# Gated cross-attention block with a mixture layer: the dense layer's rows rounded in row layout and turned by DMA transposes, logits one tile ahead

## The chip, the cores and the metric

One Trainium2 chip, one of its cores. The time is device microseconds of one execution of the whole program, input loads and output stores among them; it is the median of three executions.

## The reference, cut to what matters

```python
# x: (8, 512, 2048) f32, ctx: (8, 512, 2048) f32
x = x + tanh(g_xattn) * autocorrelation(layernorm(x), ctx, ctx)      # 8 heads, FFTs, top 12 lags
n = layernorm(x).reshape(-1, 2048)                                   # 4096 rows
base = n @ W_base.T + b_base                                         # W_base (2048, 2048)
gate = softmax(n @ W_gate.T)                                         # 8 experts
thr = sigmoid(n @ W_thr + b_thr) / 8
w = maximum(gate - thr, 0);  w = w / (sum(w) or 1)
h = einsum('nd,erd->ner', n, A_w)                                    # rank 16 for each expert
moe = einsum('ner,ne,eor->no', h, w, B_w) * 2
out = x + tanh(g_ffn) * (base + moe)
```

## The kernel before

The program has two stages in one launch. The first (the attention, to about 1545 us of the span) works through 32 steps of one batch row and 512 channels and writes the attention's result to a scratch tensor in HBM, `x2_scratch`. The change does not touch it. The second is the dense layer, and every line number below is of it.

**Weights.** `W_base`, `A_w`, `W_gate` with `W_thr`, and `B_w` are loaded in rows (into `row` and `wrow`, two 128x2048 f32 buffers each), transposed by TensorE into PSUM, and kept in SBUF as two fp16 parts each: the rounded value (`w_hi`, `ag_hi`, `b_hi`, made by ScalarE) and the remainder (`w_lo`, `ag_lo`, `b_lo`, made by VectorE). There are 19 jobs of four banks each. `ag` holds the 128 columns of `A_w`, 8 of the gate and 1 of the threshold, 137 in all.

**Tiles.** The 4096 rows are worked through in 32 tiles of 128 rows (`ROWS`), two buffers of `row` in turn. The first two and the last two tiles are written out, the others run in a loop that holds two tiles (`tiles`). There is no planner: the order on each engine is the order of the calls in its `step`. Products are taken as three fp16 products, hi·hi, hi·lo and lo·hi.

For tile i, TensorE does `logits(i)` (48 matmuls of 137 columns into `logit_bank`), `base(i)` (192 matmuls of 512 columns into the four banks of `dense`, which stay open), `turn_hw(i)` (one transpose of the gated `hw`), `turn(i + 1, 0, 2)` (8 transposes of the next tile's normalised rows into `turn_bank`), `experts(i)` (12 matmuls of 512 columns that add to `dense` and close it) and `turn(i + 1, 2, 4)` (8 more transposes). `experts(i)` needs `hwt_hi` (ScalarE) and `hwt_lo` (VectorE), both made out of the transposed `hw`. The first matmuls of `base(i)` wait, bank by bank, for `out_ready`: VectorE must have read the previous tile's result out of that bank in `finish`.

ScalarE: `gating(i)`, `normalise(i + 1, ...)` (square root, then a 128x2048 activation from `row` to `norm`), `hw_hi(i)`, `turned_hi(i + 1)` (four copies of a bank of `turn_bank` to `nt_hi`). VectorE: `gating(i)`, `statistics(i + 1, ...)`, `hw_lo(i)`, `turned_lo(i + 1, 0, 2)`, `finish(i)` (four operations, one for each bank of `dense`, into `row`), `turned_lo(i + 1, 2, 4)`. GpSimd adds the bias to `row` once tile i is normalised. SP, which issues all DMAs, in each step loads the next tile's `row` (after the store of the tile that had the buffer), waits for `out_ready`, and stores `row` to the output.

`nt_hi` and `nt_lo` have one buffer each, so they are overwritten only after `base_made`. `norm` has one buffer also.

## Time and profile before

| | |
|---|---|
| time, median of 3 executions | 3187.2 us (3184.11 to 3187.93) |
| the profiled execution | 3184.85 us |
| its span, first to last instruction | 3183.1 us |
| granted TensorE clock, mean over the span | 0.988 of full speed |
| TensorE matmul busy | 3033.0 us, 95% |
| VectorE, ScalarE, GpSimd busy | 1775.2, 873.3 and 1365.8 us |
| DMA queue q1 | 266.61 MB, 30.0% of 16 engines |

The busy time of TensorE counts each matmul to its modelled end, and matmuls overlap, so 95% is not 95% of its peak. The granted clock is 1.0 at 2.4 GHz and 0.5 at 1.2 GHz. Both stages are in the span; the shares are means over the two. In the profile's rows a line number such as L922 is a line of the kernel before.

### The profile page before, as it was taken

The numbers are of one execution on the slowest core, as the hardware profiler recorded it, in microseconds if no ns is written. First come the engines' busy times: TensorE is split into PE (matmuls) and PEld (weight loads), VectorE is DVE, ScalarE is ACT, GpSimd is POOL, SyncE is SP. The second block draws the span as 40 slices with busy tenths as digits, with TensorE's granted clock in tenths as the row PEclk, the third lists the DMA queues.
The fourth block names the chain that finished last, engine by engine and source line by source line (L and its number), as shares of the span: only waits on it lengthen the run. The fifth ranks groups of instructions, "written<-read, shape, count | busy, mean of one in ns | idle before, by whom it ended". The sixth has DMA issues, their size and how long they took to land.

```text
span 3183.1 us, 37157 instructions
## 1 busy us (share of the span) xinstructions
PE 3033.0 (95%) x13008; PEld 1569.3 (49%) x13008; DVE 1775.2 (56%) x2991; ACT 873.3 (27%) x1351; POOL 1365.8 (43%) x550
## 2 busy tenths in 40 slices
PE   4999999999999999998599999999999999999999
PEld 2545454555445455554454554545545545455454
DVE  4999999999999999888641222212212222122121
ACT  3343334333433344332421211211112112111120
POOL 4888887888888788884211101001011010110110
PEclk8999999999999999999899999999999999999999
DMA  9445544454445444431520111101101111011010
GB/s 213 124 114 124 134 111 116 121 138 105 120 122 139 104 118 113 113 83 40 219 99 27 53 40 40 53 26 53 53 26 53 40 40 53 26 53 53 26 53 27
DMA packets 130725, 267.52 MB, mean 84 GB/s; under 512 B 33705, under 2 KB 33833, under 8 KB 119881
## 3 DMA queue, kind: packets, MB, share of 16 engines
q1 hardware_dynamic: 130642, 266.61, 30.0%
q8 instruction: 28, 0.46, 0.1%
q14 instruction: 55, 0.45, 0.0%
HBM read 199.44 MB, written 67.11 MB: 84 GB/s over the span
## 4 chain that ended last, share of the span: by engine, by line
PE 50%; DMA 1%; DVE 0%; ACT 0%; issue 0%; DVEq 0%; ACTq 0%
PE bank L922 42%; PE bank L900 2%; PE bank L911 1%; PE bank L937 1%; PE bank L912 1%; PE bank L913 1%; PE bank L939 1%; PE bank L938 1%; PE bank L888 1%; DMA row<-in_L_ffn_W_base_dram 0%; DMA row<-in_L_ffn_A_w_dram 0%; DVE w_lo L1020 0%; PE bank L930 0%; DVE stats L1026 0%; ACT norm L971 0%
## 5 line engine op out<-in xcount | busy, mean ns | idle before, releaser
L1122 POOL TENSOR_TENSOR row<-row,bias 128x2048 f32<-128x2048 f32 x32 | 144.2, 4506 | 1426.8 <-ACT norm L971 1350.5
L720 POOL TENSOR_TENSOR spec_o<-spec_o,term 128x1024 f32<-128x1024 f32 x256 | 594.5, 2353 | 29.2 <-DVE term L558 29.2
L1082 DVE TENSOR_TENSOR hwt_lo<-bank,hwt_hi 128x128 f16<-128x128 f32 x32 | 9.3, 291 | 994.3 <-ACT hwt_hi L999 994.3
L922 PE MATMUL bank<-w_hi,nt_hi 128*128 128x512 f16 x2048 | 525.7, 379 | 0.0
L922 PE MATMUL bank<-w_hi,nt_lo 128*128 128x512 f16 x2048 | 525.6, 379 | 0.0
L922 PE MATMUL bank<-w_lo,nt_hi 128*128 128x512 f16 x2048 | 525.5, 379 | 0.0
L381 PE MATMUL bank<-wt,table 128*128 128x512 f32 x1024 | 448.2, 596 | 21.7 <-DVE prod_b L535 15.9
L381 PEld LDWEIGHTS bank<-wt,table 128*128 128x128 f32 x1024 | 192.2, 190 | 258.8 <-issue 229.8
L922 PEld LDWEIGHTS bank<-w_lo,nt_hi 128*128 128x128 f16 x2048 | 200.3, 98 | 241.7
L922 PEld LDWEIGHTS bank<-w_hi,nt_lo 128*128 128x128 f16 x2048 | 200.3, 98 | 241.6
L922 PEld LDWEIGHTS bank<-w_hi,nt_hi 128*128 128x128 f16 x2048 | 199.2, 98 | 234.2
L999 ACT ACTIVATE hwt_hi<-bank 128x128 f16<-128x128 f32 x32 | 8.9, 277 | 916.3 <-PE bank L930 916.3
L350 PE MATMUL bank<-qf,table 128*128 128x512 f32 x512 | 230.6, 604 | 16.2 <-POOL qf L701 13.0
L406 PE MATMUL bank<-spec_o,table 128*128 128x512 f32 x512 | 227.7, 597 | 14.6 <-POOL spec_o L720 10.9
L393 PE MATMUL bank<-table,prod_a 128*128 128x256 f32 x1024 | 229.0, 382 | 7.2 <-POOL prod_a L707 7.2
L393 PEld LDWEIGHTS bank<-table,prod_a 128*128 128x128 f32 x1024 | 196.4, 192 | 48.4 <-issue 14.8
L350 PEld LDWEIGHTS bank<-qf,table 128*128 128x128 f32 x512 | 99.2, 194 | 142.7 <-issue 141.3
L406 PEld LDWEIGHTS bank<-spec_o,table 128*128 128x128 f32 x512 | 97.8, 192 | 139.2 <-issue 123.9
L466 ACT ACTIVATE halves<-bank 128x1024 f32<-128x1024 f32 x32 | 32.7, 1023 | 454.7 <-PE bank L393 454.7
L685 POOL TENSOR_TENSOR v_sym<-vt 128x1024 f32<-128x1024 f32 x32 | 75.9, 2371 | 180.5 <-DVE corr L603 168.8
L1026 DVE BATCH_NORM_STATS2 stats<-row 128x6 f32<-128x512 f32 x124 | 76.6, 681 | 64.6 <-DMA row<-x_scratch 64.6
L701 POOL TENSOR_TENSOR qf<-xt 128x1024 f32<-128x1024 f32 x32 | 105.5, 3296 | 0.0
(149 smaller groups left out, 4428.5 us busy)
## 6 DMA issues: line engine op xcount, KB each, us to landing
xt<-in_x_dram SPq DMA_DIRECT2D x32, 1024.0 KB, 12.8
row<-x_scratch SPq DMA_DIRECT2D x32, 1024.0 KB, 4.8
out_dram<-row SPq DMA_DIRECT2D x32, 1024.0 KB, 3.9
xstat<-in_x_dram SPq DMA_DIRECT2D x28, 1024.0 KB, 10.7
vt<-in_ctx_dram SPq DMA_DIRECT2D x256, 64.0 KB
vt<-in_ctx_dram SPq DMA_DIRECT2D x64, 256.0 KB
xres<-in_x_dram SPq DMA_DIRECT2D x256, 64.0 KB
xres<-in_x_dram SPq DMA_DIRECT2D x64, 256.0 KB
```

What stands on the lines that cost most here:

```text
L350: mm = pe.matmul(pair(four, half)[:, row, :], q_tab[:, 2 * half + row, j, :], qf[:, 2 * row + j, :], start=(j == 0), stop=(j == 1))
L381: mm = pe.matmul(pair((mine, other)[y], half)[:, row, :], w_tab[:, 2 * half + row, j, :], wt[:, 2 * y + j, :], start=(j == 0), stop=(j == 1))
L393: mm = pe.matmul(four[:, ct, row * HALF:(row + 1) * HALF], prod_a[:, slot, ct * 128:(ct + 1) * 128], p_tab[:, slot, :], start=(half == 0), ...
L406: mm = pe.matmul(to[:, part, :], o_tab[:, slot, :], spec_o[:, h, slot, :], start=(row == 0), stop=(row == 1))
L466: act.activation(odd_part, four[:, :, HALF:C], ACT.Copy).then_inc(odd_copied, 1)
L685: pool.tensor_tensor(v_sym[:, 0:2, :], vt[:, 0:2, :], vt[:, 2:4, :], ALU.add).then_inc(v_symmed, 1)
L701: pool.tensor_tensor(qf[:, 2:4, :], xt[:, 0:2, :], xt[:, 2:4, :], ALU.subtract).then_inc(q_folded, 1)
L720: pool.tensor_tensor(to, to, term[:, buffer], sign).then_inc(term_added, 1)
L900: mm = pe.transpose(turn_bank[q % 2][:, k * 128:(k + 1) * 128], norm[:, d:d + 128], ident[:, :])
L922: mm = pe.matmul(dense[o][:, :], a[:, k, :], w[:, k, o * 512:(o + 1) * 512], start=(k == 0 and n == 0), stop=False)
L1026: op = dve.bn_stats(stats[:, q, :], x2[:, q * C:(q + 1) * C])
L1122: pool.tensor_tensor(row[:, par, :], row[:, par, :], bias[:, :], ALU.add).then_inc(bias_added, 1)
```

## The change

The transposes of the normalised rows leave TensorE. A tile's rows are loaded from `x2_scratch` a second time, into `norm` (`load_norm`), two tiles ahead; statistics and the normalising activation work in `norm` in place. ScalarE rounds `norm` to fp16 in row layout (`norm_hi`), GpSimd makes the remainder (`norm_lo`), and SP issues two DMA transposes, SBUF to SBUF, 128x2048 fp16 each, into `nt(par, part)`. There are two such pairs of tiles now; one pair and the two row-layout parts lie in the memory of `wrow`, which the weights no longer need by then. TensorE's step is `base(i)`, `turn_hw(i)`, `logits(i + 1)`, `experts(i)`. `turned_hi`, `turned_lo`, `turn` and `turn_bank` are gone. GpSimd adds the bias as soon as `row` is loaded. SP's steps are written out instead of looped. Left out below: renamed semaphores, the removed `turned_lo`, and unchanged lines.

```diff
@@ -750,8 +750,17 @@
             ag_hi, ag_lo = sb("ag_hi", [128, KD, NG], f16), sb("ag_lo", [128, KD, NG], f16)
             b_hi, b_lo = sb("b_hi", [128, D], f16), sb("b_lo", [128, D], f16)
             row = sb("row", [128, 2, D])
-            wrow = sb("wrow", [128, 2, D])
-            nt_hi, nt_lo = sb("nt_hi", [128, KD, 128], f16), sb("nt_lo", [128, KD, 128], f16)
+            wrow_mem = sb("wrow", [128, 2 * D])
+            wrow = wrow_mem[:, :].rearrange("p (a c) -> p a c", a=2)
+            nt_mem = sb("nt", [128, 2, KD, 128], f16)
+
+
+            spare = wrow_mem[:, :].bitcast(f16).rearrange("p (a k t) -> p a k t", a=4, k=KD)
+            norm_hi, norm_lo = (spare[:, a].rearrange("p k t -> p (k t)") for a in range(2))
+
+            def nt(par, part):
+                return spare[:, 2 + part] if par else nt_mem[:, part]
+
             bias = sb("bias", [128, D])
             ln2_scale, ln2_bias = sb("ln2_scale", [128, 1]), sb("ln2_bias", [128, 1])
             stats, mv = sb("stats2", [128, NCH, 6]), sb("mv2", [128, 2])
-            first_loaded = sem("first_loaded")
+            norm_loaded = sem("norm_loaded")
+            nt_loaded = [sem("nt_loaded0"), sem("nt_loaded1")]
+            norm_hi_made, norm_lo_made = sem("norm_hi_made"), sem("norm_lo_made")
             x2_loaded = [sem("x2_loaded0"), sem("x2_loaded1")]
             out_stored = [sem("out_stored0"), sem("out_stored1")]
-            normed, turned, nt_hi_made, nt_lo_made = sem("normed"), sem("turned"), sem("nt_hi_made"), sem("nt_lo_made")
+            normed = sem("normed")
-            dense, turn_bank, logit_bank, hw_bank = bank[0:4], bank[4:6], bank[6], bank[7]
+            dense, logit_bank, hw_bank = bank[0:4], bank[6], bank[7]
...
@@ -849,6 +860,20 @@
                     sp.dma_start(bias[:, :], b_base.rearrange("(a n) -> a n", a=1).to_broadcast([128, D])).then_inc(small_loaded, 16)
                     sp.dma_start(thr_b[:, :], b_thr.to_broadcast([128, 1])).then_inc(small_loaded, 16)
 
+                    def load_norm(i):
+                        sp.wait_ge(norm_hi_made, i)
+                        sp.wait_ge(norm_lo_made, i)
+                        sp.nop(nofuse=True)
+                        sp.dma_start(norm[:, :], x2_rows[i]).then_inc(norm_loaded, 16)
+
+                    def turn(i, par):
+                        if fleast(i) >= 2:
+                            sp.wait_ge(base_made, i - 1)
+                        for part, (source, made) in enumerate(((norm_hi, norm_hi_made), (norm_lo, norm_lo_made))):
+                            sp.wait_ge(made, i + 1)
+                            sp.nop(nofuse=True)
+                            sp.dma_start(nt(par, part), source, transpose=True).then_inc(nt_loaded[par], 16)
+
                     def load(i, par):
                         if fleast(i) >= 2:
                             sp.wait_ge(out_stored[par], 16 * (i // 2))
@@ -857,15 +882,21 @@
 
                     def step(i, par):
                         if fmost(i) + 1 < ROWS:
+                            turn(i + 1, 1 - par)
+                        if fmost(i) + 2 < ROWS:
+                            load_norm(i + 2)
+                        if fmost(i) + 1 < ROWS:
                             load(i + 1, 1 - par)
                         sp.wait_ge(out_ready, 4 * (i + 1))
                         sp.nop(nofuse=True)
                         sp.dma_start(out_rows[i], row[:, par, :]).then_inc(out_stored[par], 16)
 
-                    sp.wait_ge(wt_made, 4 * (JOBS - 1))
+                    turn(0, 0)
+                    load_norm(1)
+                    sp.wait_ge(wt_made, 4 * JOBS)
                     load(0, 0)
-                    sp.wait_ge(wt_made, 4 * JOBS)
-                    tiles(sp, step)
+                    for i in range(ROWS):
+                        step(i, i % 2)
                     for par in range(2):
                         sp.wait_ge(out_stored[par], 16 * ROWS // 2)
 
@@ -888,38 +919,24 @@
                                 mm = pe.transpose(view[:, k, :], source[0:rows, d:d + 128], ident[0:rows, 0:rows])
                             mm.then_inc(wt_made, 1)
 
-                    def turn(i, first, last):
-                        if first == 0:
-                            pe.wait_ge(normed, i + 1)
-                        for q in range(first, last):
-                            if q >= 2 or fleast(i) >= 1:
-                                pe.wait_ge(nt_hi_made, 4 * i + q - 1)
-                                pe.wait_ge(nt_lo_made, 4 * i + q - 1)
-                            for k in range(4):
-                                d = (4 * q + k) * 128
-                                mm = pe.transpose(turn_bank[q % 2][:, k * 128:(k + 1) * 128], norm[:, d:d + 128], ident[:, :])
-                            mm.then_inc(turned, 1)
-
-                    def logits(i):
+                    def logits(i, par):
                         if fleast(i) >= 1:
                             pe.wait_ge(logits_copied, i)
+                        pe.wait_ge(nt_loaded[par], 32 * (i // 2 + 1))
                         acc = logit_bank[:, 0:NG]
                         for k in range(KD):
-                            if k % 4 == 0:
-                                pe.wait_ge(nt_hi_made, 4 * i + k // 4 + 1)
-                                pe.wait_ge(nt_lo_made, 4 * i + k // 4 + 1)
-                            pe.matmul(acc, nt_hi[:, k, :], ag_hi[:, k, :], start=(k == 0), stop=False)
-                            pe.matmul(acc, nt_hi[:, k, :], ag_lo[:, k, :], start=False, stop=False)
-                            mm = pe.matmul(acc, nt_lo[:, k, :], ag_hi[:, k, :], start=False, stop=(k == KD - 1))
+                            pe.matmul(acc, nt(par, 0)[:, k, :], ag_hi[:, k, :], start=(k == 0), stop=False)
+                            pe.matmul(acc, nt(par, 0)[:, k, :], ag_lo[:, k, :], start=False, stop=False)
+                            mm = pe.matmul(acc, nt(par, 1)[:, k, :], ag_hi[:, k, :], start=False, stop=(k == KD - 1))
                         mm.then_inc(logits_made, 1)
 
-                    def base(i):
+                    def base(i, par):
                         for k in range(KD):
-                            for n, (a, w) in enumerate(((nt_hi, w_hi), (nt_hi, w_lo), (nt_lo, w_hi))):
+                            for n, (part, w) in enumerate(((0, w_hi), (0, w_lo), (1, w_hi))):
                                 for o in range(4):
                                     if k == 0 and n == 0 and fleast(i) >= 1:
                                         pe.wait_ge(out_ready, 4 * (i - 1) + o + 1)
-                                    mm = pe.matmul(dense[o][:, :], a[:, k, :], w[:, k, o * 512:(o + 1) * 512],
+                                    mm = pe.matmul(dense[o][:, :], nt(par, part)[:, k, :], w[:, k, o * 512:(o + 1) * 512],
                                                    start=(k == 0 and n == 0), stop=False)
                         mm.then_inc(base_made, 1)
 
@@ -940,18 +957,15 @@
                               .then_inc(dense_made, 1)
 
                     def step(i, par):
-                        logits(i)
-                        base(i)
+                        base(i, par)
                         turn_hw(i)
                         if fmost(i) + 1 < ROWS:
-                            turn(i + 1, 0, 2)
+                            logits(i + 1, 1 - par)
                         experts(i)
-                        if fmost(i) + 1 < ROWS:
-                            turn(i + 1, 2, 4)
 
                     pe.wait_ge(wt_hi, 4 * JOBS)
                     pe.wait_ge(wt_lo, 4 * JOBS)
-                    turn(0, 0, 4)
+                    logits(0, 0)
                     tiles(pe, step)
 
                 @block.scalar
@@ -962,22 +976,20 @@
                             act.activation(weight_target(g // 4, g % 4, 0), weight_bank(g // 4, g % 4), ACT.Copy,
                                            scale=W_SCALE).then_inc(wt_hi, 1)
 
-                    def normalise(i, x2):
+                    def normalise(i):
                         act.wait_ge(ln2_step, LN2_OPS * i + 3)
                         act.activation(std[:, :], var[:, :], ACT.Sqrt).then_inc(ln2_sqrt, 1)
                         act.wait_ge(ln2_step, LN2_OPS * (i + 1))
+                        act.activation(norm[:, :], norm[:, :], ACT.Identity, bias=ln2_bias[:, :],
+                                       scale=ln2_scale[:, :]).then_inc(normed, 1)
+
+                    def rounded(i, par):
+                        act.wait_ge(normed, i + 1)
                         if fleast(i) >= 1:
-                            act.wait_ge(turned, 4 * i)
-                        act.activation(norm[:, :], x2[:, :], ACT.Identity, bias=ln2_bias[:, :],
-                                       scale=ln2_scale[:, :]).then_inc(normed, 1)
-
-                    def turned_hi(i):
-                        if fleast(i) >= 1:
-                            act.wait_ge(base_made, i)
-                        for q in range(4):
-                            act.wait_ge(turned, 4 * i + q + 1)
-                            act.activation(nt_hi[:, 4 * q:4 * q + 4, :].rearrange("p k t -> p (k t)"),
-                                           turn_bank[q % 2][:, :], ACT.Copy).then_inc(nt_hi_made, 1)
+                            act.wait_ge(nt_loaded[1 - par], 32 * ((i - 1) // 2 + 1))
+                        else:
+                            act.wait_ge(wt_made, 4 * (NW + 1))
+                        act.activation(norm_hi, norm[:, :], ACT.Copy).then_inc(norm_hi_made, 1)
 
                     def gating(i):
                         act.wait_ge(logits_made, i + 1)
@@ -1000,16 +1012,17 @@
 
                     def step(i, par):
                         gating(i)
-                        if fmost(i) + 1 < ROWS:
-                            normalise(i + 1, row[:, 1 - par, :])
+                        if fmost(i) + 2 < ROWS:
+                            normalise(i + 2)
+                            rounded(i + 2, par)
                         hw_hi(i)
-                        if fmost(i) + 1 < ROWS:
-                            turned_hi(i + 1)
 
                     weights_hi(0, 4 * EARLY)
-                    normalise(0, norm)
+                    normalise(0)
                     weights_hi(4 * EARLY, 4 * JOBS)
-                    turned_hi(0)
+                    rounded(0, 0)
+                    normalise(1)
+                    rounded(1, 1)
                     tiles(act, step)
 
                 @block.vector
@@ -1021,9 +1034,11 @@
                                                      scalar=W_SCALE, in1=weight_target(g // 4, g % 4, 0), op0=ALU.mult,
                                                      op1=ALU.subtract).then_inc(wt_lo, 1)
 
-                    def statistics(i, x2):
+                    def statistics(i):
+                        dve.wait_ge(norm_loaded, 16 * (i + 1))
+                        dve.nop(nofuse=True)
                         for q in range(NCH):
-                            op = dve.bn_stats(stats[:, q, :], x2[:, q * C:(q + 1) * C])
+                            op = dve.bn_stats(stats[:, q, :], norm[:, q * C:(q + 1) * C])
                         op.then_inc(ln2_step, 1)
                         dve.wait_ge(ln2_step, LN2_OPS * i + 1)
                         dve.nop(nofuse=True)
...
@@ -1091,36 +1096,37 @@
 
                     def step(i, par):
                         gating(i)
-                        if fmost(i) + 1 < ROWS:
-                            dve.wait_ge(x2_loaded[1 - par], 16 * ((i + 1) // 2 + 1))
-                            dve.nop(nofuse=True)
-                            statistics(i + 1, row[:, 1 - par, :])
+                        if fmost(i) + 2 < ROWS:
+                            statistics(i + 2)
                         hw_lo(i)
-                        if fmost(i) + 1 < ROWS:
-                            turned_lo(i + 1, 0, 2)
                         finish(i, par)
-                        if fmost(i) + 1 < ROWS:
-                            turned_lo(i + 1, 2, 4)
 
                     weights_lo(0, 4 * EARLY)
-                    dve.wait_ge(first_loaded, 16)
-                    statistics(0, norm)
+                    statistics(0)
                     weights_lo(4 * EARLY, 4 * JOBS)
                     dve.wait_ge(small_loaded, 32)
                     dve.tensor_scalar(bias[:, :], bias[:, :], gates[:, 1:2], None, ALU.mult).then_inc(bias_ready, 1)
                     dve.tensor_scalar(out_gate[:, :], gates[:, 1:2], DESCALE, None, ALU.mult).then_inc(bias_ready, 1)
                     dve.tensor_scalar(thr_b[:, :], thr_b[:, :], -1.0, None, ALU.mult).then_inc(bias_ready, 1)
-                    turned_lo(0, 0, 4)
+                    statistics(1)
                     tiles(dve, step)
 
                 @block.gpsimd
                 def _(pool):
+                    def remainder(i, par):
+                        pool.wait_ge(norm_hi_made, i + 1)
+                        if fleast(i) >= 1:
+                            pool.wait_ge(nt_loaded[1 - par], 32 * ((i - 1) // 2 + 1))
+                        pool.tensor_tensor(norm_lo, norm[:, :], norm_hi, ALU.subtract).then_inc(norm_lo_made, 1)
+
                     def step(i, par):
-                        if fmost(i) == 0:
-                            pool.wait_ge(x2_loaded[0], 16)
-                        pool.wait_ge(normed, i + 1)
+                        pool.wait_ge(x2_loaded[par], 16 * (i // 2 + 1))
                         pool.tensor_tensor(row[:, par, :], row[:, par, :], bias[:, :], ALU.add).then_inc(bias_added, 1)
-
+                        if fmost(i) + 2 < ROWS:
+                            remainder(i + 2, par)
+
+                    remainder(0, 0)
+                    remainder(1, 1)
                     pool.wait_ge(bias_ready, 3)
                     tiles(pool, step)
```

## Rows read from the trace of the kernel before

**Rows 1.** Windows: us; busy PE, PEld, DVE, ACT, POOL; PEclk; DMA share; GB/s.

```profile
1560.00:1605.00 45.00, 33.95 (x257) 28.30 (x255) 41.72 (x80) 35.88 (x69) 0.00 (x0) 0.95 0.92 359
1605.00:1610.00 5.00, 4.30 (x22) 3.77 (x23) 3.25 (x6) 2.17 (x4) 3.41 (x1) 0.50 0.68 277
1613.00:3132.00 1519.00, 1517.77 (x8335) 767.06 (x8333) 351.86 (x1023) 253.41 (x403) 139.67 (x31) 1.00 0.11 42
```

**Rows 2.** Chain that ended last: start us, us, what; first, middle and last of 32.

```profile
1613.05 41.44 PE bank L922 x192
...
2397.32 41.44 PE bank L922 x192
2446.32 41.44 PE bank L922 x192
...
3132.53 41.44 PE bank L922 x192
```

**Rows 3.** Timeline of one tile's end: start us, us, engine, line, operation.

```profile
2438.59 0.27 PE L930 MATMUL bank<-ident,hw 128*128 128x128 f32 x1
...
2438.70 1.04 PE L900 MATMUL bank<-ident,norm 128*128 128x128 f32 x8
...
2439.78 0.38 PE L937 MATMUL bank<-b_hi,hwt_hi 128*128 128x512 f16 x1
...
2441.17 2.72 DVE L1089 SCALAR_TENSOR_TENSOR row<-bank,out_gate,row 128x512 f32<-128x512 f32 x4
...
2442.36 1.04 PE L900 MATMUL bank<-ident,norm 128*128 128x128 f32 x8
...
2443.24 0.22 PE L911 MATMUL bank<-ag_hi,nt_hi 128*128 128x137 f16 x1
...
2444.14 0.35 SPq L863 DMA_DIRECT2D out_dram<-row  x1
```

**Rows 4.** Timeline of the last tile's end, with nothing behind it.

```profile
3173.80 0.27 PE L930 MATMUL bank<-ident,hw 128*128 128x128 f32 x1
...
3174.55 0.29 DVE L1082 TENSOR_TENSOR hwt_lo<-bank,hwt_hi 128x128 f16<-128x128 f32 x1 [37.40 <-ACT hwt_hi L999]
...
3174.99 0.38 PE L937 MATMUL bank<-b_hi,hwt_hi 128*128 128x512 f16 x1 [0.92 <-DVE hwt_lo L1082]
...
3175.90 2.73 DVE L1089 SCALAR_TENSOR_TENSOR row<-bank,out_gate,row 128x512 f32<-128x512 f32 x4 [1.06 <-PE bank L939]
```

**Rows 5.** Timeline of a middle tile: statistics to bias.

```profile
2403.98 2.47 DVE L1026 BATCH_NORM_STATS2 stats<-row 128x6 f32<-128x512 f32 x4 [2.03 <-DMA row<-x_scratch]
...
2408.53 2.09 ACT L971 ACTIVATE norm<-row,ln_bias,ln_scale 128x2048 f32<-128x2048 f32 x1 [1.28 <-DVE ln_bias L85]
...
2410.70 4.50 POOL L1122 TENSOR_TENSOR row<-row,bias 128x2048 f32<-128x2048 f32 x1 [44.48 <-ACT norm L971]
```

**Rows 6.** Timeline of the start of the tiles.

```profile
1600.27 2.65 ACT L962 ACTIVATE ag_hi<-bank 128x512 f16<-128x512 f32 x8 [0.94 <-PE bank L888]
...
1605.05 1.94 PE L900 MATMUL bank<-ident,norm 128*128 128x128 f32 x8 [2.37 <-issue]
...
1609.37 0.32 PE L911 MATMUL bank<-ag_hi,nt_hi 128*128 128x137 f16 x1
...
1609.49 0.32 PE L912 MATMUL bank<-ag_lo,nt_hi 128*128 128x137 f16 x1
```

**Rows 7.** DMA issues: KB each, median us from issue to landing.

```profile
row<-x_scratch SPq DMA_DIRECT2D x32, 1024.0 KB, 4.8
out_dram<-row SPq DMA_DIRECT2D x32, 1024.0 KB, 3.9
...
norm<-in_L_ffn_B_w_dram SPq DMA_DIRECT2D x8, 128.0 KB, 5.6
```

**Rows 8.** Timeline of SP: the eight loads of B_w, in 64-byte runs.

```profile
47.23 13.67 SPq L299 DMA_DIRECT2D norm<-in_L_ffn_B_w_dram  x8
```

**Rows 9.** Waits of the tile loop: waited for, us in total, times, longest us.

```profile
DVE hwt_lo L1082 <- ACT hwt_hi L999: 961.4, 31, 37.4
```

More of the change, by code:

```diff
@@ L832, in x2_first @@
                         sp.wait_ge(wt_made, 4)
-                        sp.dma_start(norm[:, :], x2_rows[0]).then_inc(first_loaded, 16)
+                        sp.dma_start(norm[:, :], x2_rows[0]).then_inc(norm_loaded, 16)
                     for m in range(JOBS - 1):
@@ L1036, in statistics @@
                                ln2_scale, ln2_bias, N_SCALE)
-                    def turned_lo(i, first, last):
-                        if first == 0 and fleast(i) >= 1:
-                            dve.wait_ge(base_made, i)
-                        for q in range(first, last):
-                            dve.wait_ge(nt_hi_made, 4 * i + q + 1)
-                            dve.tensor_tensor(nt_lo[:, 4 * q:4 * q + 4, :].rearrange("p k t -> p (k t)"),
-                                              turn_bank[q % 2][:, :],
-                                              nt_hi[:, 4 * q:4 * q + 4, :].rearrange("p k t -> p (k t)"),
-                                              ALU.subtract).then_inc(nt_lo_made, 1)
                     def gating(i):
```

## The prediction, on record before the run

> **What bounds the kernel now.** I read the windows first, for the clock and the load of each engine in the tile loop. From 1613 to 3132 us TensorE is busy for 1517.8 of 1519.0 us at a granted clock of 1.00, which is the 2.4 GHz level, while VectorE has 352 us of work, ScalarE 253, GpSimd 140, and the DMA engines are 11% used [rows 1]. Then the chain that ended last: in this stretch it consists of TensorE alone, with 32 pieces of 192 base matmuls, 41.44 us each, whose starts stand 49.01 us apart (from 1613.05 to 3132.53 is 31 periods) [rows 2]. So whatever leaves TensorE's order shortens the program 31 times, and nothing else in the loop matters unless it becomes late. Third, the timeline between two pieces, to see what fills the remaining 7.6 us [rows 3]. The transpose of hw starts at 2438.59. Eight transposes of the next tile follow at 2438.70, the expert matmuls at 2439.78, eight more transposes at 2442.36, the logits at 2443.24, and the next base piece at 2446.32 [rows 2, 3]. Fourth, the last tile, which has no next tile: it shows what the short chain hw, ScalarE, VectorE, experts takes alone [rows 4].
>
> **What leaves TensorE in each tile.** Between the hw transpose's successor at 2438.70 and the experts at 2439.78 lie 1.08 us: transposes, and 0.2 us of wait for hwt_lo. The second group takes 2443.24 - 2442.36 = 0.88. Together 1.96 us. The wait does not come back: the last tile has 3174.99 - 3173.80 = 1.19 us from hw's transpose to the experts [rows 4], and the logits now stand there, which take 2446.32 - 2443.24 = 3.1 us [rows 2, 3]. They run in either order, so they cost what they did. The copies out of `turn_bank` on ScalarE and VectorE are off the chain; their going gives nothing.
>
> **What the move exposes.** Logits and the second transposes used to lie between the experts and the next base (3.96 us) and hid `finish`. Now the base follows the experts at once, and its first four matmuls wait for `out_ready`, one for each bank. In the last tile VectorE has nothing else to do, as it will have in every tile of the changed kernel: its first `finish` operation starts 3175.90 - 3174.99 = 0.91 us after the first expert matmul and the fourth ends 2.73 us later, at 3.64 [rows 4]. From VectorE's end to a waiting matmul it is another 0.15 (hwt_lo ends at 3174.84, the experts start at 3174.99). So bank 3 is free at 3.79. Without a wait the base's fourth matmul would start at 2.58 (twelve expert matmuls, 2442.36 - 2439.78) plus three times 0.215, which is 3.23. The stall is 0.56 us per tile. Its lower bound is 0.3 (no propagation, operations slightly closer), its upper one 1.0 (each of four banks handed over with its own 0.15). I take 0.56, since the last tile shows just this order. Gain per tile: 1.96 - 0.56 = 1.40 us, over 31 periods 43.4 us.
>
> **What is added beside the path.** Each tile brings a second 1 MB load into `norm`, a 2.1 us rounding on ScalarE (nearest: the 128x2048 activation, 2.09), a 4.5 us subtraction on GpSimd (nearest: its 128x2048 addition, 4.50) [rows 5], and two transposes of 512 KB. The loop moves 42 GB/s now; doubled, it is far from the 359 GB/s that the weights' stretch reached [rows 1]. The trace has no DMA transpose. Let X be the time from the issue of one to its landing. From below: a 1 MB store lands in 3.9 us, so half of that, 2 us. From above, by the runs it might be cut into: eight loads of B_w in 64-byte runs are 16384 runs (128 KB / 64 = 2048 each) and held SP for 13.67 us [rows 8]. In 256-byte runs a tile part is 2048 of them, which is 1.7 us of queue, and one such load landed in 5.6 us [rows 7]; in 32-byte runs it is 16384, 13.7 us, and about 17.6 with the 3.9 to land. Single 2-byte elements would be 262144 runs and 219 us; I keep that only as the far end. I take X = 5, nearest to the load with as many runs as 256 bytes would give.
>
> Is that hidden? Count from the first base matmul of tile i. The store of tile i-1 issues about 1.3 later (3.64 plus 0.25 as in [rows 3], minus 2.58), so the transposes of tile i+1 begin at 1.7 and land by 1.7 + 2X. Behind them on SP stand `load_norm(i + 2)`, 4.8 us [rows 7], then the load of `row`. VectorE's statistics and ScalarE's normalisation take from 2403.98 to 2410.62, 6.6 us [rows 5], and the rounding 2.1. ScalarE is then free for `hw_hi(i)`, which stands behind all this in its order, at 15.2 + 2X; so is `hw_lo` on VectorE, earlier. The hw transpose comes at 41.3, and the logits leave 3.1 - 1.2 = 1.9 us of slack behind it, so the limit is about 43.5, or X = 14.1. The logits themselves need only 1.7 + 2X < 41.4, X < 20. At X = 5 ScalarE is free at 25, and GpSimd's remainder ends at 30. VectorE already sat 961 us waiting for hwt_hi [rows 9], which is the room used. With that cover gone, the same work would cost some 8.7 us per tile on ScalarE's side plus 2X.
>
> The Trainium skill (Advanced Engine Details and Errata, X-Bar Transpose) says that such transposes are as fast as ordinary DMAs. By that X would be near the lower bound and the sum some 3 us lower. Nothing in this trace shows it.
>
> **The start.** ScalarE ends the weights at 1602.92 [rows 6]. Rounding makes it 1605.0, the remainder on GpSimd 1609.5 and some 0.3 of handing over, the second transpose X more: 1614.8. The first logits started at 1609.37. TensorE has then been idle for 12 us, so the logits run at the half clock that the window from 1605 to 1610 shows [rows 1], 0.12 us apart [rows 6], 48 of them 5.5 us, and the base starts at 1620.3 instead of 1613.05. Cost 7.3 us at X = 5, 4.3 at X = 2. The second tile's preparation (load, statistics, rounding, remainder, 2X: some 30 us) lies beside the first base. Bias, thresholds and the last tile are as before.
>
> **Sum.** Against the profiled execution, 3184.85 us (span 3183.1 and 1.75 around it): 3184.85 - 43.4 + 7.3 = 3148.7. The median of the runs is 2.35 us above that execution, so 3151.
>
> **Rivals.**
> First, slower: transposes that are cut fine. With 32-byte runs the pair holds the queue for 27.3 us and lands at 31.2 in place of 2X. ScalarE is free at 15.2 + 31.2 = 46.4, 2.9 us past the limit, in every tile; the period becomes 49.01 - 1.40 + 2.9 = 50.5, the loop 46 us longer, and the start, where the second part queues behind the first, about 29: some 3262 us. In general it decides from X = 14.5, since beyond 14.1 each us costs 2 us per tile, 62 in all. For it: nothing in the trace bounds X below that. Against: it takes eight times the runs of a 256-byte cut. Chance 0.15. The Trainium skill speaks for it (VectorE: DVE Perf Modes, The three transpose paths): it gives a DMA transpose of 128x128 at 1309 ns against 390 on TensorE. If the 16 blocks of a part came one after another, X would be 20.9 by that page and the time, an estimate, near 3590 us; no run shows it yet.
> Second, no change: `finish` eats the gain. The stall would have to be 1.7 us instead of 0.56, so the fourth `finish` would end 4.8 us after the first expert matmul. For it: in the middle tile, with VectorE busy on remainders, it ended at 2443.89, 4.1 after the experts [rows 3]. Against: those remainders go. Time about 3187. Chance 0.04.
> Third, slower by something else, GpSimd and VectorE slowing each other or a clock that falls at the new stall (0.56 us; before, a 2.4 us idle ahead of 1605 stood in front of the half clock [rows 1, 6]): 0.02.
> That the transposes do not leave TensorE can't be.
>
> **How the numbers follow.** The forecast has 0.79. Its own range: gain per tile 1.66 and start 4.3 give -47 (3140); gain 0.96 and start 16.3 at X = 14 give -13 (3174); with a little below for a stall that is smaller still, 3137 to 3174. That leaves out some 2 in 10 with the rivals, so it is the range. About 0.2%, 6.4 us, is what a measurement of this kernel can tell from no change: faster 0.80, within 0.04, slower 0.16.
>
> **What would show it.** In the changed profile: base pieces 47.6 us apart; no transposes but that of hw; logits directly behind it and no wait ahead of the experts; a wait of TensorE on `finish` of some 0.6 us; the transposes landing in about 5 us each, ScalarE waiting for the hw transpose from about 25 us into the base; the first base at about 1620. A wait of TensorE for a DMA, or of ScalarE's rounding for the transposes with the experts late behind it, would make the prediction wrong.

## The result and the profile after

The changed kernel took 3144.8 us (median of 4 runs, 3141.9 to 3146.8), the kernel before 3187.6 beside it (median of 4): ratio 0.9866, interval 0.9849 to 0.9883. It is 43 us faster. I had predicted 3151, with 3137 to 3174 as the range.

The windows of the changed kernel, in the same columns as [rows 1]: two stretches ahead of the first base, then the tile loop.

```profile
1610.00:1617.00 7.00, 0.00 (x0) 0.00 (x0) 0.00 (x0) 0.00 (x0) 3.33 (x1) 0.50 0.77 147
1617.00:1621.50 4.50, 3.67 (x33) 3.70 (x34) 0.44 (x1) 0.00 (x0) 0.00 (x0) 0.50 0.95 359
1622.80:3132.00 1509.20, 1501.91 (x8018) 728.33 (x8017) 280.42 (x909) 244.97 (x313) 269.02 (x63) 1.00 0.29 86
```

TensorE is still the engine that is always busy, at the full clock, but it now idles 7.3 us in the loop where it idled 1.2. GpSimd's work doubled from 140 to 269 us, VectorE's fell, and the DMA traffic doubled to 86 GB/s. None of that is on the chain: VectorE is there with `finish` alone. This is the chain (start us, us, what; it answers [rows 2]):

```profile
1622.76 41.44 PE bank L939 x192
1667.99 2.74 DVE row L1094 x4
1670.78 40.97 PE bank L939 x189
...
2428.24 2.04 DVE row L1094 x3
2430.33 40.97 PE bank L939 x189
2477.79 40.97 PE bank L939 x189
...
3094.93 40.97 PE bank L939 x189
```

The pieces have 189 matmuls instead of 192, because the chain now enters the base at its fourth matmul, by way of VectorE's `finish` (L1094). From 1670.78 to 3094.93 is 30 periods of 47.47 us, against 49.01. The timeline of a tile's end shows both halves of that, and answers [rows 3].

```profile
2471.13 0.27 PE L947 MATMUL bank<-ident,hw 128*128 128x128 f32 x1
...
2474.16 0.38 PE L954 MATMUL bank<-b_hi,hwt_hi 128*128 128x512 f16 x1
...
2476.75 0.81 PE L939 MATMUL bank<-w_hi,nt 128*128 128x512 f16 x3
2477.79 0.39 PE L939 MATMUL bank<-w_hi,nt 128*128 128x512 f16 x1 [0.23 <-DVE row L1094]
```

And VectorE in the same stretch:

```profile
2475.01 2.73 DVE L1094 SCALAR_TENSOR_TENSOR row<-bank,out_gate,row 128x512 f32<-128x512 f32 x4 [2.84 <-PE bank L956]
```

Between hw's transpose and the experts lie 3.03 us, filled by the logits without a wait. Three base matmuls follow the experts at once; the fourth would start at 2474.16 + 3.23 = 2477.39 and starts at 2477.79. That is a stall of 0.40 us. (The 0.23 in the row counts only from the modelled end of the third matmul, and some 30 of these are the 7.3 us of idle in the window above; what a tile loses is the 0.40 between the starts.) `finish` begins 0.85 after the first expert matmul and ends at 3.58, and TensorE goes on 0.05 later.

The start of the tiles, answering [rows 6]:

```profile
1604.69 2.60 ACT L976 ACTIVATE ag_hi<-bank 128x512 f16<-128x512 f32 x8 [0.61 <-PE bank L919]
...
1607.18 1.90 ACT L992 ACTIVATE wrow<-norm 128x2048 f16<-128x2048 f32 x1
...
1609.16 6.18 SPq L875 DMA_TRANSPOSE nt<-wrow  x2
1609.16 4.17 POOL L1120 TENSOR_TENSOR wrow<-norm,wrow 128x2048 f16<-128x2048 f32 x1 [77.63 <-ACT wrow L992]
...
1617.83 0.28 PE L928 MATMUL bank<-ag_hi,nt 128*128 128x137 f16 x1 [10.79 <-DMA nt<-wrow]
```

Rounding, remainder and second transpose follow one another, and TensorE waits 10.8 us. (The row of SP joins both issues, 1.85 and 1.93 us, with the wait for the remainder between them.) The DMA issues of the whole run (KB where given, median us to landing; [rows 7]) price what the trace before could not:

```profile
norm<-x_scratch SPq DMA_DIRECT2D x32, 1024.0 KB, 5.6
row<-x_scratch SPq DMA_DIRECT2D x32, 1024.0 KB, 7.0
out_dram<-row SPq DMA_DIRECT2D x32, 1024.0 KB, 4.4
nt<-wrow SPq DMA_TRANSPOSE x32, 4.5
wrow<-wrow SPq DMA_TRANSPOSE x32, 4.4
```

A median hides two cases here. The two transposes issued at 2430.78 and 2435.5, least, median and most:

```profile
DMA to landing us min/median/max: 4.3/5.4/6.6
```

The first of a pair, issued 0.4 us behind the output store, lands after 6.6 us and the second after 4.3. Ahead of the first base, with no store in front, both land after 4.3 to 4.4. So 4.4 us is the time of a 512 KB transpose by itself, and a pair in the loop takes 9.0 us from its first issue to its last landing. The packets under 512 bytes rose from 33705 to 167321, which is 2088 for each of the 64 transposes: runs of 256 bytes (512 KB / 256 = 2048).

Put together: 31 periods by 1.54 us are 47.7 us gained, and from the end of the weights' copies on ScalarE to the first base it is 15.5 us (1607.3 to 1622.8) instead of 10.1 (1602.9 to 1613.05), 5.4 lost. The net, 42.3, fits the difference of the medians, 42.8. The two profiled spans differ by 38.1 only, because in the changed kernel's execution the weights' copies ended 4.4 us later, in code that the change does not touch; 3 us of that were there already when the weights began. That point moves from run to run: the same copies end at 1603.8 us in plain and at 1610.3 in one_nt, two of the runs below.

### The profile page after: what moved, and what is told of

It reads as the page before. It is cut to its first block, busy times and chain, and to the rows that moved or that the text cites. A ratio compares the mean times of both kernels' runs of the same rounds, so it can differ in the third digit from the quotient of the medians.

```text
span 3145.0 us, 35465 instructions
## 1 busy us (share of the span) xinstructions
PE 2976.3 (95%) x12496; PEld 1510.2 (48%) x12496; DVE 1699.9 (54%) x2863; ACT 861.7 (27%) x1253; POOL 1494.1 (48%) x582
## 2 busy tenths in 40 slices
DMA packets 268310, 333.59 MB, mean 106 GB/s; under 512 B 167321, under 2 KB 167449, under 8 KB 253497
## 4 chain that ended last, share of the span: by engine, by line
PE 46%; DVE 3%; DMA 1%; issue 1%; ACT 0%; POOL 0%; DVEq 0%; ACTq 0%; SPq 0%
PE bank L939 42%; DVE row L1094 2%; PE bank L928 1%; PE bank L929 1%; PE bank L930 1%; PE bank L919 1%; DMA row<-in_L_ffn_W_base_dram 1%; DMA row<-in_L_ffn_A_w_dram 0%; PE bank L956 0%; PE bank L954 0%; PE bank L955 0%; DVE w_lo L1033 0%; DMA nt<-wrow 0%; POOL wrow L1120 0%; PE bank L947 0%
## 5 line engine op out<-in xcount | busy, mean ns | idle before, releaser
L1120 POOL TENSOR_TENSOR wrow<-norm,wrow 128x2048 f16<-128x2048 f32 x32 | 130.3, 4071 | 1230.2 <-ACT wrow L992 1230.2
L939 PE MATMUL bank<-w_hi,wrow 128*128 128x512 f16 x2048 | 489.3, 379 | 3.8 <-DVE row L1094 3.8
L939 PE MATMUL bank<-w_hi,nt 128*128 128x512 f16 x2048 | 489.0, 379 | 3.5 <-DVE row L1094 3.5
L939 PEld LDWEIGHTS bank<-w_hi,wrow 128*128 128x128 f16 x2048 | 200.2, 98 | 251.7 <-DVE row L1094 13.7
L939 PEld LDWEIGHTS bank<-w_hi,nt 128*128 128x128 f16 x2048 | 200.6, 98 | 250.3 <-DVE row L1094 12.7
L939 PE MATMUL bank<-w_lo,wrow 128*128 128x512 f16 x1024 | 262.8, 379 | 0.0
L939 PE MATMUL bank<-w_lo,nt 128*128 128x512 f16 x1024 | 262.8, 379 | 0.0
L1041 DVE BATCH_NORM_STATS2 stats<-norm 128x6 f32<-128x512 f32 x128 | 79.1, 681 | 310.1 <-DMA norm<-x_scratch 310.1
L939 PEld LDWEIGHTS bank<-w_lo,nt 128*128 128x128 f16 x1024 | 100.4, 98 | 118.9
```

Source lines behind the costliest of these rows:

```text
L939: mm = pe.matmul(dense[o][:, :], nt(par, part)[:, k, :], w[:, k, o * 512:(o + 1) * 512], start=(k == 0 and n == 0), stop=False)
L1041: op = dve.bn_stats(stats[:, q, :], norm[:, q * C:(q + 1) * C])
L1120: pool.tensor_tensor(norm_lo, norm[:, :], norm_hi, ALU.subtract).then_inc(norm_lo_made, 1)
```

## The experiments

**Put the transposes back (work_back).** Sixteen f32 transposes a tile return to TensorE, of the identity, into banks that nothing reads; it is work that no output needs.

```diff
                         for k in range(KD):
+                            pe.transpose(bank[4 + k // 8][:, 0:128], ident[:, :], ident[:, :])
                             for n, (part, w) in enumerate(((0, w_hi), (0, w_lo), (1, w_hi))):
```

> The changed kernel with 16 transposes of the identity, f32 128x128, put back on TensorE in each tile, one ahead of each k of the base matmuls, into two banks that nothing reads. My theory: the gain is TensorE's time for the 16 removed transposes. They cost 0.11 us each (eight in 0.87 us before), so the base starts should stand 47.47 + 1.75 = 49.2 us apart, and the time should be 3144.8 + 32 x 1.75 = 3201 us, slightly above the kernel before. Rival: the gain is the waits that went, or a lighter ScalarE and VectorE; then the transposes fit in somewhere and the period stays below 48.

Measured: 3197.2 us, ratio to before 1.0034 (1.0022 to 1.0047). Two stores of neighbouring tiles are issued at 2406.81 and 2455.92, a period of 49.1. The gain was TensorE's time and went back with it.

**The order alone (order_only).** The kernel before, with `nt` in two pairs and the transposes on TensorE moved into the base.

```diff
-                        logits(i)
-                        base(i)
-                        turn_hw(i)
-                        if fmost(i) + 1 < ROWS:
-                            turn(i + 1, 0, 2)
-                        experts(i)
-                        if fmost(i) + 1 < ROWS:
-                            turn(i + 1, 2, 4)
+                        base(i, par)          # turn(i + 1, q, q + 1) ahead of k = 8, 10, 12, 14
+                        turn_hw(i)
+                        if fmost(i) + 1 < ROWS:
+                            logits(i + 1, 1 - par)
+                        experts(i)
```

> The kernel before with only the order changed: TensorE still makes the 16 transposes (four each in the middle of the base matmuls), nt has two pairs of tiles, and the logits run one tile ahead between hw's transpose and the experts. No DMA transpose, no second load. My theory: the order alone is worth the 0.2 us wait for hwt_lo and costs the 0.41 us wait for finish, so the period is about 47.47 + 1.75 = 49.2 us against 49.01, and the time 3187 + 6 = 3193 us. Rival: running the logits ahead is what gives the gain; then the period falls to about 48 and the time to 3155.

Measured: 3193.4 us, ratio 1.0023 (1.0013 to 1.0033). The fourth base matmuls of two tiles, with the wait that the new order brings:

```profile
2401.85 0.39 PE L932 MATMUL bank<-w_hi,nt 128*128 128x512 f16 x1 [0.27 <-DVE row L1099]
2451.07 0.39 PE L932 MATMUL bank<-w_hi,wrow 128*128 128x512 f16 x1 [0.23 <-DVE row L1099]
```

The period is 49.22, against 49.01. The order by itself, with TensorE's transposes moved into the base as it needs them, gains nothing; it costs 0.2 us a tile.

**Logits behind the experts, and logits cut in two (logits_last, split).**

```diff
                         turn_hw(i)
+                        experts(i)
                         if fmost(i) + 1 < ROWS:
                             logits(i + 1, 1 - par)
-                        experts(i)
```

```diff
                         turn_hw(i)
                         if fmost(i) + 1 < ROWS:
-                            logits(i + 1, 1 - par)
+                            logits(i + 1, 1 - par, 0, 8)
                         experts(i)
+                        if fmost(i) + 1 < ROWS:
+                            logits(i + 1, 1 - par, 8, KD)
```

> The changed kernel with the logits of the next tile behind the experts instead of ahead of them. My theory: the wait for hwt_hi and hwt_lo comes into the open (1.19 us from hw's transpose to the experts, less 0.11 for the transpose itself, 1.08), and the wait for finish, 0.41 us, is hidden by the logits. The period is 47.47 + 1.08 - 0.41 = 48.14 us and the time 3144.8 + 21 = 3166 us. Rival: the place of the logits does not matter; period 47.5, time 3145.

Measured: 3165.9 us, ratio 0.9932 (0.9915 to 0.9948). Its base pieces start 48.14 us apart, and the wait is the other one:

```profile
2436.96 0.38 PE L954 MATMUL bank<-b_hi,hwt_hi 128*128 128x512 f16 x1 [0.91 <-DVE hwt_lo L1087]
```

> The changed kernel with the logits cut in two: 24 of the 48 matmuls ahead of the experts (1.46 us, enough for the 1.08 us of the hw chain) and 24 behind them (1.47 us, enough for the 0.41 us wait for finish). My theory: both waits are hidden, the period is 41.4 + 0.1 + 2.9 + 2.6 = 47.05 us and the time 3144.8 - 13 = 3132 us. Rival: the wait of the base on finish isn't VectorE's being late but a cost of any semaphore wait there; then the period stays at 47.4.

Measured: 3133.6 us, ratio 0.9830 (0.9814 to 0.9846); run again with the last experiment, 3132.9 and 0.9828 (0.9814 to 0.9841). The chain is TensorE alone again:

```profile
2470.79 41.44 PE bank L941 x192
2517.85 41.44 PE bank L941 x192
```

A period of 47.06 us, no wait at either place. The stall on `finish` was VectorE's being late by 0.41 us, and no cost of the wait as such: half of the logits covers each wait.

**Are the transposes hidden, and up to what price (turn3, turn5, plain)?**

```diff
+                        for again in range(1, REPEAT):
+                            sp.wait_ge(nt_loaded[par], 32 * (REPEAT * (i // 2) + again))
+                            for part, source in enumerate((norm_hi, norm_lo)):
+                                sp.nop(nofuse=True)
+                                sp.dma_start(nt(par, part), source, transpose=True).then_inc(nt_loaded[par], 16)
```

> The changed kernel with each pair of DMA transposes made three times, each repeat issued when the pair before has landed. In the changed kernel ScalarE is done with the rounding 22.5 us after the base's first matmul, and its limit by the prediction is 43.5 us. A pair takes 6.6 us to issue and some 2 more to land, so two more pairs are 17 us: ScalarE is done at 39.5. My theory: hidden; period 47.5 us, and only the first tile pays, 17 us: time 3162 us. Rival: DMA transposes cost TensorE or the other transfers something in proportion; then the period rises by some tenths of a us or more.

Measured: 3156.7 us, ratio 0.9900 (0.9883 to 0.9917). From 2585.94 its base pieces start 47.47 us apart, as in the changed kernel, and from the first base matmul to the last tile's fourth it is 1472.4 us (1635.78 to 3108.14) against 1472.2 (1622.76 to 3094.93). Three times the transposes cost the loop nothing. Only the first tile pays: from the issue of the first transpose to the first logits it is 22.2 us (1607.94 to 1630.10) instead of 8.7, 13.5 more. I had expected 17, at 8.5 for a further pair, which takes 6.8. The medians differ by 12.

> The changed kernel with each pair of DMA transposes made five times, one after the other. Four more pairs are some 34 us: ScalarE would be done with the rounding at 56.5 us, 13 past the limit of 43.5, with the experts late behind hw_hi. My theory: period 60.5 us, first tile 34 us later, time 3144.8 + 31 x 13 + 34 = 3582 us, and TensorE's wait stands ahead of the experts, not ahead of the logits. Rival: there is no such limit (the engines run further ahead than one tile); period below 50.

Measured: 3412.8 us, ratio 1.0705 (1.0687 to 1.0723). The limit is there and in the expected place. First SP, behind the store at 2433.32 that follows; then ScalarE and TensorE at the end of the tile whose base began at 2377.54:

```profile
2433.76 6.88 SPq L875 DMA_TRANSPOSE wrow<-wrow  x2
2443.00 25.10 SPq L880 DMA_TRANSPOSE wrow<-wrow  x8
2468.21 0.70 SPq L867 DMA_DIRECT2D norm<-x_scratch  x1
```

```profile
2425.69 1.91 ACT L997 ACTIVATE wrow<-norm 128x2048 f16<-128x2048 f32 x1 [0.16 <-ACT norm L988]
2427.50 0.26 ACT L1016 ACTIVATE hwt_hi<-bank 128x128 f16<-128x128 f32 x1
```

```profile
2419.36 0.27 PE L952 MATMUL bank<-ident,hw 128*128 128x128 f32 x1
2428.30 0.59 PE L959 MATMUL bank<-b_hi,hwt_hi 128*128 128x512 f16 x1 [5.74 <-DVE hwt_lo L1092]
```

ScalarE rounds until 50.1 us into the base, and `hw_hi` goes only then, though hw was transposed at 41.8. TensorE waits 5.74 us ahead of the experts, and for the 3 us behind that it runs at the half clock (granted 0.50 from 2428 to 2431 us), so that the experts take 3.98 us instead of 2.59. The period is 54.7 (fourth base matmuls at 2433.31 and 2488.00), 7.2 over 47.47; taking off 1.4 for the clock, the limit lay at 50.1 - 5.8 = 44.3 us. My expectation of 13 late was wrong in the price of the repeats: a further pair takes 6.8 us, as in turn3, and the norm's load waits for the issue of the last pair, not for its landing. The load goes out 34.9 us after the store (2433.32 to 2468.21), where in the changed kernel it is 7.15 (2430.34 to 2437.49): 27.7 more, not 34.

> The changed kernel with plain SBUF to SBUF copies of the same tiles in place of the DMA transposes, so that nt holds rows that are not turned. It shows what the turning costs a DMA. My theory: the transposes are hidden, so the period stays 47.47 us whatever a copy takes; a copy issues in about 0.4 us instead of 2 to 6 and lands in about 3.5, and the first base starts some 2 us sooner. Time 3143 us. Rival: the transposes slow something in the loop (TensorE's reads, the load of norm); then the period falls by 0.1 us or more.

The output is that of rows that are not turned. Measured: 3143.0 us, ratio 0.9861 (0.9844 to 0.9877), period 47.46 (2426.66 to 2474.12). From 2400 to 2890 us its copies and loads:

```profile
norm<-x_scratch SPq DMA_DIRECT2D x10, 1024.0 KB, 8.4
...
nt<-wrow SPq DMA_DIRECT2D x10, 512.0 KB, 5.6
wrow<-wrow SPq DMA_DIRECT2D x10, 512.0 KB, 5.5
```

These medians, too, lie between two cases, and the two issued at 2427.11 and 2427.7 show them:

```profile
DMA to landing us min/median/max: 4.7/5.5/6.4
```

Here the first lands after 4.7 us and the second, issued 0.6 us behind it, after 6.4. SP issues a pair in 1.9 us instead of 6.6, and the pair has landed 7.0 us after its first issue, against 9.0 for the transposes. Norm's load then waits in the queue and lands after 8.4 instead of 5.6. With no store in front the difference is seen on one DMA. The chain ahead of the first base, in plain and then in the changed kernel:

```profile
1605.70 5.01 POOL wrow L1120
1610.77 3.20 DMA nt<-wrow
1619.08 41.44 PE bank L939 x192
```

```profile
1609.16 4.18 POOL wrow L1120
1613.40 4.29 DMA nt<-wrow
1622.76 41.44 PE bank L939 x192
```

A copy lands 1.1 us sooner than a transpose of the same 512 KB. Yet the first base came hardly sooner, and there I was wrong by 2 us: 15.5 us after the end of A_w's and the gate's transposes (1603.58 to 1619.08), against 15.7. Most of the 1.1 us went to GpSimd's remainder, which took 0.8 us longer in this execution, because it overlapped longer with an operation of VectorE (last section).

**One pair of nt (one_nt).** The cover taken away.

```diff
-                return spare[:, 2 + part] if par else nt_mem[:, part]
+                return nt_mem[:, part]
@@
-                        if fleast(i) >= 2:
-                            sp.wait_ge(base_made, i - 1)
+                        if fleast(i) >= 1:
+                            sp.wait_ge(base_made, i)
```

> The changed kernel with one pair of nt tiles instead of two, so that the next tile's transposes wait for the end of the base. Everything that was hidden behind the base stands in the open then: two transposes 6.6 us to issue, norm's load 5.6 more, statistics and normalisation 6.6, rounding 1.9, hw_hi and hw_lo 0.8, in all 21.5 us from the end of the base to the experts. My theory: period 41.4 + 21.5 + 2.6 + 0.4 = 66 us, time 3144.8 + 31 x 18.5 = 3718 us. Rival: only the transposes come into the open, 8.8 us less the experts' chain: period about 55, time 3380 us.

Measured: 3715.8 us, ratio 1.1650 (1.1631 to 1.1669). The base pieces from 1691.31 to 3015.38 are 20 periods of 66.2 us. Part of its chain, from the hw transpose (2394.28) on, start us, us, what:

```profile
2399.19 5.48 DMA norm<-x_scratch
...
2409.29 2.10 ACT norm L983
...
2413.72 0.30 DVE hwt_lo L1087
...
2414.16 0.59 PE bank L954
```

20 us stand between hw's transpose and the experts, and the clock adds to it (granted 0.88 of full speed in the loop; in this tile 0.50 for the experts, which take 5.07 us instead of 2.59). The 66 that I expected had a wait of 21.5 and no clock in it, so the close hit, 3718 against 3715.8, is partly luck. The double buffer, not a cheap transpose, is what makes the change pay.

**The first tile sooner (split_early).** On top of split:

```diff
-                    weights_hi(4 * EARLY, 4 * JOBS)
-                    rounded(0, 0)
+                    weights_hi(4 * EARLY, 4 * (NW + 1))
+                    rounded(0, 0)
+                    weights_hi(4 * (NW + 1), 4 * JOBS)
```

> The kernel with the logits cut in two, and the first tile's rounding moved ahead of ScalarE's last eight weight copies, so that it runs while TensorE waits for A_w. In the changed kernel the rounding started at 1607.18, right after those copies; here it can start about 3 us sooner, and GpSimd's remainder, the second transpose and the first logits follow it. My theory: everything behind the start is a shift of 3 us, period 47.06 us, time 3133.6 - 3 = 3130.6 us. Rival: the copies of A_w and the gate, 1.9 us later now, hold up TensorE or VectorE by as much; no gain, 3133.6 us.

> The kernel with the logits cut in two once more, on the same chip as the one above, for the difference between them: 3133.6 us, the other 3 us below it if the first tile's start is what it gains.

Measured: 3128.6 us, ratio 0.9815 (0.9801 to 0.9828), and split beside it 3132.9. From A_w's first transpose to the first logits it is 10.1 us (1600.23 to 1610.31), and 14.4 in split_again (1602.88 to 1617.31), 4.3 less. Of that 3.6 arrive at the first base (15.2 to 1615.42, and 18.8 to 1621.66), since the logits, begun earlier, had the half clock for longer: 38 of 48 matmuls against 24. I had expected 3. The medians differ by 4.3, but the two intervals overlap, so the traces carry this claim more than the times do. This version is the fastest here, 58 us below the kernel before.

## Why the prediction was right

**What leaves TensorE: 1.96 us predicted.** The period and the stall give 49.01 - 47.47 + 0.40 = 1.94. work_back returned 1.64 of it (49.11 - 47.47) as transposes; the rest is the wait of 0.2 for hwt_lo and 0.1 of the stall, which the first added transpose covers (work_back's first four base matmuls take 1.32 us with the stall and 1.03 without). order_only excludes the rival reading that the order gains.

**The stall on finish: 0.56 predicted, 0.40 measured.** The last tile was the right place to read it, but two terms were large: `finish` started 0.85 after the first expert matmul and not 0.91, and the hand-over to TensorE took 0.05, not the 0.15 that I took from hwt_lo. logits_last and split show the mechanism from both sides. So the gain per tile was 1.54 instead of 1.40, 4.3 us over 31 periods; this is the term that was off most.

**The transposes: X = 5 predicted, 4.4 measured** without a store in front, 6.6 and 4.3 for a pair behind one, so 9.0 where the prediction had 2X = 10; and 256-byte runs, as the row of B_w's loads suggested. The limit that I worked out, ScalarE free by 43.5 us, was 44.3 in turn5; the changed kernel has it free about 22.6 us into the base (normalisation from 2447.75 on, 2.09 and 1.91 us behind a base from 2429.28), sooner than my 25, since norm's load does not wait for the transposes to land. The rival of fine cuts is out by the packets. The Trainium skill says that such transposes are as fast as ordinary DMAs (Advanced Engine Details and Errata, X-Bar Transpose). In this case they were near it and slower: 4.3 against 3.2 us to the landing, 9.0 against 7.0 for a pair in the loop, and 6.6 against 1.9 for its issue on SP. The Trainium skill's 1309 ns for a 128x128 block (VectorE: DVE Perf Modes, The three transpose paths) can't be added up block by block: 16 blocks landed in 4.4 us, not in 20.9.

**The start: 7.3 us predicted, 5.4 measured.** Rounding 1.9 (2.1), remainder 4.17 (4.5), transpose and hand-over 4.5 (5.3), and the clock rose before the last logits, so that all took 4.8 us instead of 5.5 (48 at 0.12 would have been 5.8). The steps and their order were right, and each was priced a little too high.

The sum was 36 us of gain and the medians show 43: 4.3 of the difference is the gain per tile, 1.9 the start. Both errors point the same way, so nothing cancelled. The 0.15 for the slow rival was not foolish by what the trace before had, since nothing in it bounded X; by the experiments the slack is (44.3 - 22.6) / 6.8, some three further pairs of transposes: with two the program was still faster than before, with four it was slower. The third rival, GpSimd and VectorE slowing each other, was given 0.02; it is real, as the last section shows, but comes once, at the start: in the loop GpSimd's remainder took 4.06 to 4.07 us in each of 28 tiles.

## What to carry to other kernels

When an engine is the bound in every tile, count its removed instructions by start-to-start time and add what they were hiding: here 1.96 us went and 0.4 came back, because the matmuls that moved had covered the reading of the accumulators. Independent work on the bounding engine is best cut so that a piece lies in front of each wait; half of the logits on either side of the experts was worth another 11 us. A slow step can be taken off a busy engine, here at up to three times its latency, if it has a second buffer and most of a period of slack. But look at what stands behind it in order on the other engines, since that is where it becomes late.

## What the runs showed that I had not expected

A wait of 5.7 us on TensorE costs more than itself. In turn5 it waited from 2422.6 us on; the granted clock was still 1.00 up to 2426 and was 0.50 for the 3 us behind the wait, which cost 1.4 us in this tile. A stall of 0.4 us left it at 1.00.

VectorE's scaling of the bias and GpSimd's remainder, both over 128x2048 f32, meet at the start of the tiles, and which of them begins first decides which is long. In split_again GpSimd is ahead by 0.08 us:

```profile
1608.82 5.05 DVE L1112 TENSOR_SCALAR bias<-bias,gates 128x2048 f32<-128x2048 f32 x1
```

```profile
1608.74 4.05 POOL L1124 TENSOR_TENSOR wrow<-norm,wrow 128x2048 f16<-128x2048 f32 x1 [76.43 <-ACT wrow L996]
```

In plain VectorE is ahead by 0.18:

```profile
1605.52 1.27 DVE L1108 TENSOR_SCALAR bias<-bias,gates 128x2048 f32<-128x2048 f32 x1
```

```profile
1605.70 5.00 POOL L1120 TENSOR_TENSOR wrow<-norm,wrow 128x2048 f16<-128x2048 f32 x1 [75.04 <-ACT wrow L992]
```

The one that begins first takes its ordinary time (1.26 to 1.28 us, and 4.05 to 4.07 as in the loop); the other takes longer by the time that they overlap, less some 0.15 us. The other runs fit: GpSimd took 4.17 us with an overlap of 0.26 in the changed kernel and 4.79 with 0.86 in split, and VectorE took 5.06 in turn3 and turn5, where it began 0.08 us second. Where GpSimd is the late one it is on the chain, up to 0.9 us of the start. No run moves the one operation alone, so that these two exclude each other rests on this pattern.
